# Gated-feature attention: another order for its round of score tiles, turns, features, exponentials and value products

## The reference, cut to what matters

```
def _psi(x, proj_w, proj_b):
    gen = x @ proj_w.T + proj_b
    A, Bg = (gen[..., 0:8], gen[..., 8:16])
    Th = jnp.clip(gen[..., 16:24], -8.0, 8.0)
    psi_real = A * jnp.exp(Th) + Bg * jnp.cos(Th)
    psi_imag = Bg * jnp.sin(Th)
...
tensor = jnp.einsum('bhqd,bhkd->bhqk', qr, kr) + jnp.einsum('bhqd,bhkd->bhqk', qi, ki)
spinor = jnp.einsum('bhqd,bhkd->bhqk', qr, ki) - jnp.einsum('bhqd,bhkd->bhqk', qi, kr)
gram = qn2[..., :, None] * kn2[..., None, :]
wedge = jnp.sqrt(jnp.maximum(gram - tensor ** 2 - spinor ** 2, 0.0) + 1e-06)
scores = (geo_w[0] * wedge + geo_w[1] * tensor + geo_w[2] * spinor + geo_w[3] * hodge) / 4.0
w = jax.nn.softmax(scores / temperature, axis=-1)
out = jnp.einsum('bhqk,bhkd->bhqd', w, Vh)
return out @ Wo_w.T + Wo_b
...
x = _layernorm(x + _L1_xattn_ref(x, ctx_1024, ctx_1024, ...), axis=-1)
```

## Time and profile before

| | us |
|---|---|
| median of three runs | 2825.59 (2822.96 to 2841.47) |
| the profiled execution, its time | 2834.78 |
| its span, first to last instruction | 2833.1 |
| of it, from the first score tile of psi to its last norm (2057.99 to 2580.48) | 522.5 |
| of these, ACT busy | 417.9 |
| PE busy | 403.6 |
| DVE busy | 331.4 |

### The profile page before, as it was taken

One profiled execution on the slowest core, in us unless ns is written; L12 is line 12 of the kernel. 1 busy time (PEld: TensorE's weight loads), 2 busy tenths in 40 slices (PEclk: granted clock), 3 DMA queues, 4 the chain that ended last, 5 costly groups with the idle time before them and its releaser, 6 DMA issues. The chain is left out here.

```text
span 2833.1 us, 32030 instructions
## 1 busy us (share of the span) xinstructions
PE 2371.9 (84%) x11624; PEld 1503.3 (53%) x11624; DVE 1695.8 (60%) x3500; ACT 1363.7 (48%) x1968; POOL 325.7 (11%) x299
## 2 busy tenths in 40 slices
PE   6888888876888888887999699997568878777998
PEld 4656666652333333334566456565355655555886
DVE  5666666624666666654643598989566666743232
ACT  2333333311555555562222565654188888782221
POOL 0000000000000000000156400000111111100000
PEclk7999999966999999999899899998789999998999
DMA  2000000006333333214034512111200000002000
GB/s 77 8 16 15 16 16 15 8 8 165 53 68 68 61 66 57 47 27 162 16 59 65 106 38 68 45 68 46 102 8 31 30 31 30 23 15 75 15 23 23
DMA packets 104949, 132.46 MB, mean 47 GB/s; under 512 B 21748, under 2 KB 87556, under 8 KB 104792
## 3 DMA queue, kind: packets, MB, share of 16 engines
q1 hardware_dynamic: 90440, 115.58, 15.2%
q0 software_dynamic: 11904, 14.69, 3.2%
q10 hardware_dynamic: 2448, 0.14, 0.1%
HBM read 73.69 MB, written 31.20 MB: 37 GB/s over the span
## 5 line engine op out<-in xcount | busy, mean ns | idle before, releaser
L987 DVE TENSOR_REDUCE xattn_tops<-region 128x2 f32<-128x1024 f32 x256 | 306.3, 1220 | 128.9 <-PE region L771 128.8
L924 ACT ACTIVATE xattn_probs<-region 128x1024 f32<-128x1024 f32 x256 | 256.3, 1022 | 126.1 <-PE region L760 125.0
L156 PE MATMUL region<-gla_xT,weights_even 128*128 128x512 f32 (+1 forms) x416 | 200.6, 637 | 21.0 <-ACT gla_xT L248 21.0
L760 PE MATMUL region<-xattn_qs,xattn_ks 49*128 49x512 f32 x512 | 126.6, 496 | 61.8 <-DVE xattn_tops L987 31.4
L156 PE MATMUL region<-mamba_xT,weights_odd 128*128 128x512 f32 x320 | 156.4, 636 | 3.1 <-DVE mamba_xh L1988 3.1
L2491 DVE CUSTOM_DVE_ANT_0 weights_even<-psi_wedge,region,psi_unsign 128x512 f32<-128x512 f32 x128 | 95.4, 746 | 98.9 <-ACT psi_wedge L2325 97.3
L156 PEld LDWEIGHTS region<-gla_xT,weights_even 128*128 128x128 f32 (+1 forms) x416 | 77.1, 192 | 133.9 <-issue 107.0
L789 PE MATMUL region<-xattn_probs,xattn_va 128*32 128x512 f32 x1024 | 142.6, 624 | 1.4 <-ACT xattn_o_T L951 1.4
L771 PE MATMUL region<-xattn_ks,xattn_qs 48*128 48x512 f32 x512 | 126.5, 493 | 13.0 <-DMA xattn_ks<-xattn_khi 8.6
L165 PE MATMUL region<-weights_even,gla_work 128*128 128x256 f32 x512 | 119.6, 394 | 17.6 <-DVE gla_work L631 11.0
L760 PEld LDWEIGHTS region<-xattn_qs,xattn_ks 49*128 49x128 f32 x512 | 48.9, 190 | 141.0 <-DVE xattn_tops L987 70.8
(11 more groups left out here) (534 smaller groups left out, 5377.4 us busy)
## 6 DMA issues: line engine op xcount, KB each, us to landing
weights_even<-mamba_cs SPq DMA_DIRECT2D x32, 512.0 KB, 4.7
xattn_qs<-xattn_qhi SPq DMA_DIRECT2D x128, 64.0 KB, 2.3
xattn_ks<-xattn_khi SPq DMA_DIRECT2D x128, 64.0 KB, 2.3
moe_sums<-moe_picked SPq DMA_DIRECT2D x9, 512.0 KB, 7.8
gla_x<-in_x SPq DMA_DIRECT2D x8, 512.0 KB, 3.8
x_after_gla<-gla_res SPq DMA_DIRECT2D x8, 512.0 KB, 2.9
xattn_x<-x_after_gla SPq DMA_DIRECT2D x8, 512.0 KB, 4.1
xattn_ctxT<-in_ctxT SPq DMA_DIRECT2D x8, 512.0 KB, 4.4
```

The source lines that it names most:

```text
L156: last = st.nc.tensor.matmul(o[0:m, i, :], w[:, c, col + i * P:col + i * P + m], rhs[:, c, :], start=c == 0, stop=c == kc - 1)
L760: last = mm(o[:, r, :], ks[rows, ring(n), a, j * P:j * P + P], qs[rows, ring(n), a, :], start=True, stop=True)
L924: A_(probs[:, p % 3, a, :, :], st.region(f"k{v}")[:], ACT.Exp).then_inc(st.emptying(f"k{v}"), 1)
L987: V.tensor_reduce(tops[:, n % 2, t, a::2], st.region(f"q{u}")[:], AX, ALU.max).then_inc(st.emptying(f"q{u}"), 1)
```

## The change

The list is written in another order, and four small pieces of code move with it:

- DVE's least of a tile becomes a step of its own ("least"), most of them one tile behind the score; the entry "score 16", which held the last one, goes.
- The turns of heads 2 and 3, the feature turns 4 to 6, the transposes of x and features 2 to 4 with split 0 stand together between tiles 4 and 5. Features 0 goes to the end of the round before.
- pv 1 and both scaled move from the middle of the score tiles behind tile 15; pv 0 moves from behind the first tile of the next round to the end of the round, ahead of fT 3; the reciprocal ("recip") is taken at the round's end. `out` stands between turns 1 and 2, residual and norm behind it.
- Sin stands ahead of the exponentials.
- fT 1 and 2 are copied by DVE in place of ACT.
- The norm is applied by POOL in place of DVE.

The end of the list for a round, and the code:

```
                 yield "score", b, 15
-                yield "angles", b + 2, 3
+                yield "least", b, 14
+                yield "sin", b + 2, 0
                 yield "exp", b, 0
...
-                yield "turn", b, 3
-                yield "sin", b + 2, 0
+                yield "features", b + 2, 0
+                yield "recip", b, 0
+                yield "pv", b, 0
                 yield "fT", b + 1, 3
...
-                    elif what == "fT":
+                    elif what == "fT" and i not in (1, 2):
                         act.wait_ge(*st.full(f"fT{b}_{i}"))
...
-                        else:
-                            A_(fK[0:64, 0::2, :], o[0:64, :, :], ACT.Copy)
-                            last = A_(fK[64:P, 1::2, :], o[64:P, :, :], ACT.Copy)
...
+                    if what == "least":
+                        dve.wait_ge(st.sem("wedge_root"), GQ * b + i + 1)
...
+                    elif what == "fT" and i in (1, 2):
+                        dve.wait_ge(*st.full(f"fT{b}_{i}"))
...
+                        if i == 1:
+                            V.tensor_copy(fL[0:64, 0, :], o[0:64, 0, :])
+                            V.tensor_copy(fL[64:P, 1, :], o[64:P, 0, :])
+                            last = V.tensor_copy(fQ[:, 0, :], o[:, 1, :])
+                        else:
+                            V.tensor_copy(fK[0:64, 0::2, :], o[0:64, :, :])
+                            last = V.tensor_copy(fK[64:P, 1::2, :], o[64:P, :, :])
+                        last.then_inc(st.emptying(f"fT{b}_{i}"), 1)
+                    elif what == "recip":
                         dve.wait_ge(st.sem("exped"), GH * (b + 1))
...
-                        norm.vector(dve, nth, x, x, "x_out")
+                        if b:
+                            dve.wait_ge(st.sem("x_out"), b)
+                        norm.moments(dve, nth, x)
...
                         norm.gpsimd(pool, nth, K["neg_half"], 1e-5)
+                        x = xs[b % XS]
+                        pool.wait_ge(st.sem("rstd0"), b + 1)
+                        for t in range(NT):
+                            last = G.tensor_scalar(x[:, t, :], x[:, t, :], norm.mv[:, t, 0:1], norm.rstd[:, t:t + 1],
+                                                   ALU.subtract, ALU.mult)
+                        last.then_inc(st.sem("x_out"), 1)
```

More of the change, by code:

```diff
@@ L2089, in order @@
+                yield "features", b + 1, 4
+                yield "split", b + 1, 0
                 yield "score", b, 5
-                yield "features", b + 1, 3
+                yield "Q", b + 2, 0
                 yield "score", b, 6
-                yield "fT", b, 6
+                yield "least", b, 5
                 yield "score", b, 7
+                yield "least", b, 6
+                yield "features", b + 1, 5
+                yield "gen", b + 2, 0
                 yield "score", b, 8
-                yield "features", b + 1, 4
@@ L2096, in order @@
-                yield "Q", b + 2, 0
+                yield "least", b, 7
                 yield "score", b, 9
-                yield "scaled", b - 1, 0
-                yield "split", b + 1, 0
-                yield "features", b + 1, 5
+                yield "least", b, 8
+                yield "features", b + 1, 6
+                yield "angles", b + 2, 0
                 yield "score", b, 10
-                yield "pv", b - 1, 1
-                yield "features", b + 1, 6
+                yield "least", b, 9
@@ L2104, in order @@
+                yield "split", b + 1, 1
                 yield "score", b, 11
-                yield "split", b + 1, 1
-                yield "gen", b + 2, 0
+                yield "least", b, 10
+                yield "angles", b + 2, 1
                 yield "score", b, 12
-                yield "scaled", b - 1, 1
-                yield "angles", b + 2, 0
+                yield "least", b, 11
+                yield "angles", b + 2, 2
                 yield "score", b, 13
-                yield "angles", b + 2, 1
+                yield "least", b, 12
@@ L2119, in order @@
+                yield "scaled", b - 1, 0
+                yield "scaled", b - 1, 1
                 yield "fT", b + 1, 0
                 yield "exp", b, 1
-                yield "score", b, 16
+                yield "fT", b + 1, 1
+                yield "turn", b, 0
+                yield "turn", b, 1
+                yield "out", b - 1, 0
+                yield "exp", b, 2
+                yield "fT", b + 1, 2
                 yield "residual", b - 1, 0
                 yield "norm", b - 1, 0
-                yield "turn", b, 0
@@ L2177, in _ @@
                         last.then_inc(st.filling(f"fT{b}_{i}"), 1)
-                    elif what == "score" and i < GQ:
+                    elif what == "score":
                         h, t = divmod(i, NT)
@@ L2484, in _ @@
                 for what, b, i in work:
[L2485 to L2492, removed]
-                                                   low[:, b % 2, j:j + 1]).then_inc(st.emptying(f"s{b}_{j}"), 1)
+                    if what == "least":
+                        dve.wait_ge(st.sem("wedge_root"), GQ * b + i + 1)
+                        if i % NT == 0 and b:
+                            dve.wait_ge(*st.full(f"pT{b - 1}_{i // NT}_1"))
+                        V.tensor_tensor_reduce(scores[:, i, :], wedge[:, i % 2, :], st.region(f"s{b}_{i}")[:, 1, :],
+                                               unsign[:], 1e30, ALU.add, ALU.min, low[:, b % 2, i:i + 1]).then_inc(
+                                                   st.emptying(f"s{b}_{i}"), 1)
                     elif what == "features":
```

34 lines of the change are left out of this document (20 added, 14 removed).

## The result

The changed kernel takes 2923.48 us (median of 4 runs, 2904.86 to 2928.12), the kernel before, beside it on the same chip, 2833.53 (4 runs): ratio 1.0324, interval 1.0282 to 1.0366. It is slower by some 90 us, where 39 were forecast. The profiled execution of after has 2928.12 us (span 2926.4), 93 more than that of before.

A forecast was written before the change was run, and what follows sets the result against it. No engine was full; ACT was nearest to a bound, busy 53.99 of a 64.83 us round. Order at full clock +19 and clock +20 gave +39 on the median 2825.59, so 2865 us, range 2838 to 2888.

The forecast's parts named there:

- the chain: Exponentials' phase: `out`, turn 2's casts, residual, moments, two copies, pv 0, fT3 make ACT wait 9.9 us; +6.0 a round.
- the walk at full clock: Middle round laid out without clock loss: score phase 42.0 against 44.12, exponentials' phase 26.75 against 20.71, together 68.8 us.
- ahead of the first tile: Start of the psi stage: one table load more, +1.2 us.
- first round: No `out`, residual or moments: second phase 20.2, first about 41, together 61.2 us, +2.3.
- five middle rounds: Rounds of 68.8 us each make 343.8 against 326.77: +17 us.
- seventh round: No Q, gen or angles: phases about 34.5 against 41.03 and 24.8 against 19.7, -1.4 us.
- last round and tail: Score phase 32.2 against 36.38, pv 0 about 2.6 later, POOL's applying some 1.5 longer: 0.
- clock: PE slow at two places of the exponentials' phase, pv 0 (1.6) and turn 1 with `out` (1.2): 2.8 a round, +20 us.
- Rival 2: Both thin places of the exponentials' phase run slow to the end: 5.7 a round, +59, 2885 us; chance 0.12.
- Rival 1: PE's clock does not fall in the new order: +19, 2845 us; chance 0.22.
- Rival 3: Value products covered, DVE's copy of turn 3 done by 11.2 us, exponentials' phase 16.95: about 2783 us; chance 0.06.
- Rival 4: Score phase loses its waits for Q, gen and angles (5.4 us): about 2818, 2838 with the clock; chance 0.07.

The follow-up runs named there:

- e1: Changed kernel with the first half of the value product (pv 0) put back behind the next batch's first score tile: 2867.44 us, ratio 1.0159 to the kernel before.
- e2: Changed kernel with DVE's layer-norm moments moved behind the copies of turns 2 and 3: 2903.81 us, ratio 1.0283 to the kernel before.
- f2: Changed kernel with pv 1 behind score tile 9 and `out` right behind the last score tile, pv 0 unmoved: 2869.19 us, ratio 1.0150 to the kernel before.
- e3_fill: Changed kernel with extra matmuls at six places where PE idled, in both phases: 2887.86 us, ratio 1.0207 to the kernel before.
- f4_before_fill: Kernel before with 14 extra matmuls a round where PE waited for the sums' reciprocal: 2826.12 us, ratio 0.9986.
- g4_sin_back: Changed kernel with Sin back behind the exponentials and features 0 behind the next batch's first tile: 2889.05 us, ratio 1.0169 to the kernel before.
- g3_before_casts: Kernel before with only feature turns 1 and 2 copied by DVE, norm still applied by DVE: 2827.66 us, ratio 0.9994.
- f3_all_late: Changed kernel with `out` early, pv 0 behind the next batch's second score tile, moments behind the copies: 2829.14 us, ratio 1.0010 to the kernel before.

## Why the prediction was wrong

**Right: the chain.** ACT waits for turn 3 of the features, released by PE; pv 0 waits for DVE's copy; the copies of turns 2 and 3 lie behind the moments; the clock falls in that phase. e1, e2 and f2 each took one link out, and ACT's 14.40 us fell to 6.90, 12.94 and 8.13.

**Right in size: the walk at full clock, per round.** Exponentials' phase 26.75 forecast, 27.69 in e3_fill, 26.9 by the estimate without its fill; score phase 42.0 forecast, 43.96 in e3_fill, 42.4 by the estimate without the meeting of POOL and DVE. DVE's casts were priced at 1.16 each, from the pT copies; they took 1.22. By the rule on PSUM sources in the Trainium skill's page "VectorE: DVE Perf Modes", section "Why PSUM operands drop a tier", that was the value to take, and the trace agrees.

The miss is 51 us (90 less 39). e3_fill and f4_before_fill split the stage's 91 us into some 55 for the order and 36 for the clock:

| part of the stage | forecast at full clock | measured, filled runs |
|---|---|---|
| ahead of the first tile | +1.2 | +5.5 |
| first round | +2.3 | +10.9 |
| five middle rounds | +17 | +32.0 |
| seventh round | -1.4 | +4.5 |
| last round and tail | 0 | +2.6 |
| clock | +20 | +36 |

The clock's 36 is 91.0 less the 55.5 of the rows above it. By the estimates above the clock's part is larger: 2.3 us of each middle round of e3_fill, some 11 of the 32.0, come from its fill and from POOL's addition, which after meets in one of these rounds.

**The step that failed first, and by the estimates the largest: the clock was charged in one phase only.** It makes 16 of the missing 51 by the table, some 27 by the estimates. 2.8 us a round were put at two places of the exponentials' phase, and the score phase was walked as if at full clock. Its place was in the forecast's own rows: the sums' wait and the slow turn behind it. Before, it ended with that turn, and spread behind it ran at full speed:

```profile
2325.16 1.96 PE L2222 MATMUL region<-psi_recipT,ident 16*64 16x128 f32 x32
```

After, it goes on:

```profile
2375.24 1.91 PE L2212 MATMUL region<-ident,weights_even 128*128 128x128 f32 x8
2377.08 3.68 PE L2238 MATMUL region<-psi_recipT,ident 16*64 16x128 f32 x32
2380.68 1.97 PE L2212 MATMUL region<-ident,weights_even 128*128 128x128 f32 x8
```

Spread takes 3.68 us where it took 1.96, and ACT waits 2.59 for it, 0.7 forecast. Why PE stays slow longer than before is not shown: its wait ahead of the sums is 2.51 us here and was 3.93. The exponentials' phase itself lost 4.2 by the rows for 2.8 (turn 1 0.7, `out` 0.95, pv 0 2.6): pv 0 2.6 and not 1.6 over, since it was slow from end to end. Rival 2, that both places run slow to the end, put 5.7 a round; with the score phase's share the whole was at least 6.9 in the round shown.

**The second step: two small misses a round, five times.** By e3_fill, 0.9 and 2.0 us in the two phases make 15 of the missing 51. The gain of 2.1 in the score phase was not reached: with fill it is 43.96, the 44.12 of before. But 0.75 of the 0.9 is the fill's, and 1.55 of the 2.0 goes with POOL's addition meeting DVE's features, which the walk did not have. So by the estimate the walk itself was off by some 0.6 us a round, and of these 15 us most are the clock's.

**The third step: the ends were estimated, not walked.** They make 21 of the missing 51. Sin ahead of the exponentials was costed as a table load, 1.2. In the stage's start ACT waits at Sin for DVE's angles of the second batch, and the first batch's feature copies are queued behind it:

```profile
2058.55 0.63 ACT L2317 ACTIVATE psi_prods<-psi_prods 128x512 f32<-128x512 f32 x1 [11.59 <-DVE psi_prods L2481]
...
2060.82 1.00 ACT L2325 ACTIVATE psi_fA<-region 128x1024 fp32r<-128x1024 f32 x1
```

With Sin put back (g4_sin_back) 1.8 us of this came back; the casts of turn 2 on DVE, costed at nothing here, are another part: in g3_before_casts the two turns' casts alone add 2.0 ahead of the first tile (56.8 for 54.8).

In the first round no turns of a batch before cover DVE's block of features 2 to 4 and split, and POOL's addition meets this block: one DVE operation takes 2.87 us for 0.68 (2074.52). ACT waits 4.25 us for features 4 ahead of Q's copy, and 3.95 and 5.24 for the tiles behind it; "about 41" for the first phase was 46.4 (2065.16 to the Sin table at 2111.58), and 47.1 with fill, so that it is not the clock. In the seventh round the phases were 36.3 and 25.9 with fill, 34.5 and 24.8 forecast; the rest of its 5.9 is that fill takes 3.1 us off this round in the kernel before. At the end pv 0 starts 5.9 us after the last exponential (2642.36 and 2636.44), before 0.3, where 2.6 later was forecast; POOL's four last operations take 4.83 us where DVE's took 1.38, 3.5 more where 1.5 was forecast.

**Rivals.** Rival 1 (the clock does not fall) is out by the 0.81. Rival 3 (faster) asked for turn 3's copy by 11.2 us; f3_all_late had a phase without ACT waits by other means, and its gain was used up in the score phase. Rival 4 is out: the waits for Q (1.60 us), tile 8 (2.02) and tile 10 (2.33) are there, as walked (1.5, 2.1 and 2.4).

## What to carry to other kernels

Moving a step away from the engine that looks fullest did not pay here where what replaced it was queued on two other engines between that engine's last work and its next: the same two moves gained 0.5% in the old order and came with a loss of 3.2% in the new one. When an order makes PE wait, look for slow rows behind its waits in every phase and not only where the change is, and walk the first and the last round too, since the cover of the middle rounds is missing there. Steps put into one block can also release another engine's work into it, as the transposes of x did with POOL's addition. Extra matmuls in PE's idle places are a cheap way to tell a clock's share from an order's, if what they hold up themselves is taken off.

## What was not expected of the hardware

POOL's norm operation, 128x256 with two scalars a partition, took 1.2 us each (4.83 for four), where 0.6 to 1 was estimated from the earlier trace rows. Beside it DVE's features ran on, only stretched: four 128x256 operations in SBUF took 0.41, 0.41, 0.42 and 0.58 us from 2437.47 on, and POOL's four took 5.26.

```profile
2436.84 5.26 POOL L2578 TENSOR_SCALAR psi_x<-psi_x,psi_mv,psi_rstd 128x256 f32<-128x256 f32 x4
```

The Trainium skill's page "SBUF — State Buffer", section "SBUF: two separate sides", describes the port pair that both share as an exclusive lock, with the second instruction blocked until the first ends. By that a DVE operation with two SBUF inputs would have waited up to 1.2 us beside each of these; the rows show 0.24 at most (0.66 for 0.42), and the rows decide. Beside POOL's addition to x, which reads two operands in SBUF, the rows are as the page has it:

```profile
2073.96 2.88 POOL L2568 TENSOR_TENSOR psi_x<-psi_x,rows 128x1024 f32<-128x1024 f32 x1 [1.15 <-PE region L148]
2074.52 2.87 DVE L2395 TENSOR_TENSOR psi_prods<-psi_z,psi_zk 128x512 f32<-128x512 f32 x1
```

The DVE operation, 0.68 us alone, takes 2.87 and ends 0.55 us behind POOL's. The earlier trace rows had such a pair too: 3.11 us for an operation that takes 1.09 alone. Why POOL's two kinds of operation differ in this is not shown.
